# Four-layer sequence block: residual sums on TensorE and ScalarE and a new order in the routing stage

## The reference

```python
x = L0_attn_x                                                # (16, 256, 128)
x = x + attention(layernorm(x), Wqkv, bqkv, Wout, bout)      # softmax, 16 heads of 8
x = x + recurrent(layernorm(x), wf, uf, bf, wi, ui, bi, wc, uc, bc, wo, uo, bo, in_c)
x = x + linear_attention(layernorm(x), w_qkv, w_out)         # rope, elu + 1 features, 16 heads
x = x + experts(layernorm(x), Wr, br, W1, b1, W2, b2)        # the best two of 16 experts
```

```python
def step(c, xt):
    ft = sigmoid(xt @ wf.T + c @ uf.T + bf)
    it = sigmoid(xt @ wi.T + c @ ui.T + bi)
    gt = tanh(xt @ wc.T + c @ uc.T + bc)
    return ft * c + it * gt, None
h = tanh(x @ wo.T + c_final @ uo.T + bo)
```

```python
logits = x @ Wr + br
w, idx = top_k(softmax(logits), 2); w = w / sum(w)
y = sum over the two of w * (gelu(x @ W1[e] + b1[e]) @ W2[e] + b2[e])
```

## Time and profile before

| | |
|---|---|
| median of 3 runs | 697.38 us (693.48 to 697.74) |
| profiled execution | 696.24 us, its span 694.4 us |
| TensorE busy | 505.3 us, 73% of the span |
| VectorE busy | 432.5 us, 62% |
| GpSimd busy | 392.0 us, 56% |
| ScalarE busy | 348.8 us, 50% |

### The profile page before, as it was taken

The page is one execution under the profiler, slowest core; times in us unless marked ns, Lnnn a source line. Parts: engine busy times, 40 slices in busy tenths (PEclk is TensorE's granted clock), DMA queues, the critical chain, the costliest instruction groups (busy, mean ns, idle before and its releaser), DMA issues.

```text
span 694.4 us, 15346 instructions
## 1 busy us (share of the span) xinstructions
PE 505.3 (73%) x4146; PEld 345.2 (50%) x4146; DVE 432.5 (62%) x1259; ACT 348.8 (50%) x765; POOL 392.0 (56%) x692
## 2 busy tenths in 40 slices
PE   1468899999999999876777776766514776977730
PEld 0224555555555555444455555544414776877620
DVE  5467888888788888422478888887543344443306
ACT  1027777777777777752256545553322443444310
POOL 4555777776777753433215676677760665556550
PEclk9999999999999999997599999998555998989875
DMA  2864444343343331000700000000022222222119
GB/s 73 229 151 107 110 118 103 96 100 98 105 105 92 100 97 48 5 1 1 248 0 24 26 27 27 23 31 29 31 74 67 79 79 69 72 79 67 56 30 342
DMA packets 64092, 55.91 MB, mean 81 GB/s; under 512 B 8462, under 2 KB 56739, under 8 KB 64035
## 3 DMA queue, kind: packets, MB, share of 16 engines
q1 hardware_dynamic: 57986, 46.03, 25.0%
q0 software_dynamic: 4608, 8.47, 3.7%
q10 hardware_dynamic: 1440, 0.73, 0.4%
HBM read 30.53 MB, written 25.71 MB: 81 GB/s over the span
## 4 chain that ended last, share of the span: by engine, by line
PE 17%; issue 10%; POOL 7%; DVE 6%; another core or an unknown queue 3%; ACT 3%; DMA 3%; SPq 2%; POOLq 1%; DVEq 0%; ACTq 0%
PE p_qkv L1680 5%; POOL disp L1027 3%; POOL root L1045 2%; PE p_u L1693 1%; DMA own<-back 1%; PE p_kvo L1693 1%; PE p_qkv L1439 1%; ACT hid L1653 1%; PE p_r L1693 1%; PE p_qkv L1440 1%; PE p_h L1693 1%; POOL gap L1072 1%; DVE t L1133 1%; PE p_u L1447 1%
## 5 line engine op out<-in xcount | busy, mean ns | idle before, releaser
L422 DVE TENSOR_REDUCE negmax<-p_dve 128x4 f32<-128x1024 f32 x128 | 155.9, 1221 | 42.9 <-PE p_dve L612 41.5
L515 ACT ACTIVATE probs<-p_exp 128x1024 f32<-128x1024 f32 x128 | 130.7, 1021 | 28.4 <-PE p_exp L589 27.9
L1567 POOL DMA_INDIRECT back<-XN2T,rows x80 | 80.9, 1012 | 73.1 <-DVE XN2T L1627 49.0
L1027 POOL DMA_INDIRECT disp<-pay,pos x64 | 67.2, 1051 | 36.5 <-issue 18.4
L603 PE MATMUL p_out<-probs,V 128*32 128x256 f32 x1024 | 68.5, 385 | 0.0
L1653 ACT ACTIVATE hid<-p_qkv,own 128x128 f32<-128x128 f32 x160 | 45.6, 372 | 36.6 <-PE p_qkv L1680 16.6
L612 PE MATMUL p_dve<-KS,QS 61*128 61x256 bf16 x512 | 52.6, 287 | 13.1 <-DVE negmax L422 8.1
L1680 PE MATMUL p_qkv<-XN2T,own 128*128 128x128 f32 x320 | 48.4, 300 | 13.0 <-ACT XN2T L1645 10.1
L589 PE MATMUL p_exp<-QS,KS 64*128 64x256 bf16 x512 | 50.8, 277 | 8.5 <-ACT probs L515 4.4
L1680 PEld LDWEIGHTS p_qkv<-XN2T,own 128*128 128x128 f32 x320 | 44.3, 214 | 15.1 <-issue 13.5
L1619 DVE COPY own<-expert 128x514 f32 x80 | 35.7, 447 | 12.0 <-issue 11.9
(11 more groups left out here) (246 smaller groups left out, 1281.1 us busy)
## 6 DMA issues: line engine op xcount, KB each, us to landing
scratch<-part SPq DMA_DIRECT2D x32, 192.0 KB, 2.1
KS<-scratch SPq DMA_DIRECT2D x32, 192.0 KB, 3.3
QS<-scratch SPq DMA_DIRECT2D x32, 192.0 KB, 4.3
rows<-disp SPq DMA_DIRECT2D x80, 65.0 KB
scratch<-part SPq DMA_DIRECT2D x32, 128.0 KB, 2.0
own<-back SPq DMA_DIRECT2D x8, 512.0 KB, 6.6
expert<-in_W_dram SPq DMA_DIRECT2D x1, 2064.0 KB, 8.9
scratch<-part SPq DMA_DIRECT2D x32, 64.0 KB, 1.9
```

Of the source, the lines that this page charges most:

```text
L422: dve.tensor_reduce(negmax[q][:, i, :, 2 * hp:2 * hp + 2], p_dve[buf][:, :].rearrange("p (v w k) -> p v w k", v=HALF, k=S), AX.X, ALU.max, ...
L515: act.activation(probs[s % 4][:, :, :, :].rearrange("p v w q -> p (v w q)"), p_exp[:, :], ACT.Exp)\
L1027: pool.indirect_dma_start(out=disp, out_offset=bass.IndirectOffsetOnAxis(ap=pos[q][:, i, k:k + 1], axis=0), in_=pay[q][:, k, i, :], in_off ...
L1567: pool.indirect_dma_start(out=back, out_offset=bass.IndirectOffsetOnAxis(ap=rows[r][:, h, D + 1:ROW].bitcast(U32), axis=0), in_=y[r][:, h, :],
```

## The change

Eight edits, six of them in the routing stage:
1. The seven later loads of stage 1 are issued by ScalarE behind its first copies of q and k, no longer by SyncE.
2. In slot 2 of stage 1, where no attention weights are left to apply, TensorE does the blocks for VectorE before those for ScalarE.
3. `pipeline()` of the routing stage writes all turns out; there is no hardware loop.
4. `gap` is gone: ScalarE makes the exponential from `best` itself, one instruction for each of the two token tiles, with the second value as bias and the first scaled by -1.
5. `sent` becomes two semaphores, one for each set of buffers, and GpSimd no longer waits for the scatters of the turn before.
6. `uoh` is made by VectorE, no longer by GpSimd.
7. Both residual sums are made in the bank: TensorE multiplies with the identity instead of transposing, and adds X as a second product with the identity. ScalarE copies the sum from the bank to X. VectorE's two adds are gone.
8. Every engine has a new order in a turn.

```diff
+            def later_loads():
+                act.dma_start(X[:, 8:2 * B, :], t["x_dram"].rearrange("(n p) d -> p n d", p=P)[:, 8:2 * B, :]).then_inc(x_in[3].sem, 16)
+                act.dma_start(bo[:, :], t["bout"].partition_broadcast(P)).then_inc(w_in.sem, 16)
+                act.dma_start(Wout[:, :], t["Wout"]).then_inc(w_in.sem, 16)
...
+                        if at(n, 0):
+                            later_loads()
...
-                    for_act(n, r, s)
-                    for_dve(n, r, s)
+                    if s == 2 and not active(n, 2):
+                        for_dve(n, r, s)
+                        for_act(n, r, s)
+                    else:
+                        for_act(n, r, s)
+                        for_dve(n, r, s)
...
-        x4T_p, x4T_s, lg_p, lg_s, gap_s, odds_s = sig("x4T_p"), sig("x4T_s"), sig("lg_p"), sig("lg_s"), sig("gap_s"), sig("odds_s")
+        x4T_p, x4T_s, lg_p, lg_s, odds_s = sig("x4T_p"), sig("x4T_s"), sig("lg_p"), sig("lg_s"), sig("odds_s", TT)
         top_s, hot_s, pay_s = sig("top_s", 4), sig("hot_s"), sig("pay_s", 2)
-        rank_p, pos_s, sent = sig("rank_p"), sig("pos_s", 4), sig("sent", 16 * TT * TOP)
+        rank_p, pos_s = sig("rank_p"), sig("pos_s", 4)
+        sent = [sig(f"sent{q}", 16 * TT * TOP) for q in range(PAIR)]
...
-            peel = deepest + PAIR
-            rounds = (B - peel) // PAIR
-            for n in range(peel):
-                iteration(n, n % PAIR)
-            with eng.Fori(0, rounds, 1) as k:
-                for c in range(PAIR):
-                    iteration(k * PAIR + (peel + c), (peel + c) % PAIR)
-            for n in range(peel + rounds * PAIR, B + deepest):
+            for n in range(B + deepest):
...
-            pool.tensor_scalar(uoh[:, :], w["uo"][:, :], 0.5, None, ALU.mult).then_inc(s2.sem, 1)
...
-                                        in_=pay[q][:, k, i, :], in_offset=None).then_inc(sent.sem, 16)
+                                        in_=pay[q][:, k, i, :], in_offset=None).then_inc(sent[q].sem, 16)
...
-                    if sent.due(b - 1):
-                        pool.wait_ge(sent.sem, sent.at(b - 1))
                     steady(pool, t)
                     scatter(o, 0, 0)
+                root_power(n, r)
                 if active(n, 5):
                     scatter(o, 0, 1)
-                root_power(n, r)
                 if active(n, 5):
                     scatter(o, 1, 0)
                 if active(n, 5):
                     scatter(o, 1, 1)
                 if active(n, 4):
                     b = n - 4
-                    pool.wait_ge(top_s.sem, top_s.at(b, TT))
-                    if odds_s.due(b - 1):
-                        pool.wait_ge(odds_s.sem, odds_s.at(b - 1))
-                    pool.tensor_tensor(gap[:, :], best[:, :, 1], best[:, :, 0], ALU.subtract).then_inc(gap_s.sem, 1)
+                    pool.wait_ge(nm4.sem, nm4.at(b))
+                    steady(pool, t)
+                    pool.tensor_tensor(X[:, bass.ds(2 * b, 2), :], X[:, bass.ds(2 * b, 2), :], pay[r][:, 0, :, 0:D], ALU.add)\
+                        .then_inc(res.sem, 1)
                 if active(n, 4) and not (isinstance(n, int) and n - 4 < PAIR):
                     b = n - 4
-                    pool.wait_ge(sent.sem, sent.at(b - PAIR))
+                    pool.wait_ge(sent[b % PAIR].sem, sent[b % PAIR].at(b // PAIR - 1))
                     steady(pool, t)
                     pool.tensor_scalar(pay[r][:, :, :, D + 1].bitcast(I32), pay[r][:, :, :, D + 1].bitcast(I32), float(PAIR * TOP * TT), None, ALU.add)\
                         .then_inc(ids_up.sem, 1)
-                if active(n, 5):
-                    b = n - 5
-                    pool.wait_ge(nm4.sem, nm4.at(b))
-                    steady(pool, t)
-                    pool.tensor_tensor(X[:, bass.ds(2 * b, 2), :], X[:, bass.ds(2 * b, 2), :], pay[o][:, 0, :, 0:D], ALU.add)\
-                        .then_inc(res.sem, 1)
 
             pipeline(pool, iteration, 5)
             then["pool"](pool)
...
+                    dve.wait_ge(w["loaded"].sem, w["loaded"].at(0))
+                    dve.tensor_scalar(uoh[:, :], w["uo"][:, :], 0.5, None, ALU.mult).then_inc(mv_set.sem, 1)
...
-                    dve.tensor_tensor(X[:, bass.ds(2 * b, 2), :], p_u[:, 0:S].rearrange("p (i d) -> p i d", i=TT), X[:, bass.ds(2 * b, 2), :], ALU.add)\
-                        .then_inc(x3_s.sem, 1)
...
-                    dve.tensor_tensor(X[:, bass.ds(2 * b, 2), :], p_h[:, 0:S].rearrange("p (i d) -> p i d", i=TT), X[:, bass.ds(2 * b, 2), :], ALU.add)\
-                        .then_inc(x2_s.sem, 1)
...
-                    act.wait_ge(gap_s.sem, gap_s.at(b))
...
+                if active(n, 1):
+                    b = n - 1
+                    act.wait_ge(hT_p.sem, hT_p.at(b))
+                    if at(b, 0):
+                        act.wait_ge(s2.sem, 4)
+                        act.wait_ge(fill_set.sem, fill_set.at(0))
+                    act.activation(X[:, bass.ds(2 * b, 2), :], p_h[:, 0:S].rearrange("p (i d) -> p i d", i=TT), ACT.Identity,
+                                   bias=w["fill"][:, 0:1], scale=KVones[0][:, 0, D:D + 1]).then_inc(x2_s.sem, 1)
...
+                    act.wait_ge(top_s.sem, top_s.at(b, TT))
                     if gate_in.due(b - 1):
                         act.wait_ge(gate_in.sem, gate_in.at(b - 1))
-                    act.activation(odds[:, 1, :], gap[:, :], ACT.Exp).then_inc(odds_s.sem, 1)
+                    for i in range(TT):
+                        act.activation(odds[:, 1, i:i + 1], best[:, i, 0:1], ACT.Exp, bias=best[:, i, 1:2], scale=-1.0).then_inc(odds_s.sem, 1)
...
+                    act.wait_ge(u_p.sem, u_p.at(b))
+                    act.wait_ge(nm3.sem, nm3.at(b))
+                    act.activation(X[:, bass.ds(2 * b, 2), :], p_u[:, 0:S].rearrange("p (i d) -> p i d", i=TT), ACT.Identity,
+                                   bias=w["fill"][:, 0:1], scale=KVones[0][:, 0, D:D + 1]).then_inc(x3_s.sem, 1)
...
+                    pe.wait_ge(onT3_s.sem, onT3_s.at(b))
+                    pe.wait_ge(x2_s.sem, x2_s.at(b))
+                    if x3_s.due(b - 1):
+                        pe.wait_ge(x3_s.sem, x3_s.at(b - 1))
+                    for i in range(TT):
+                        pe.matmul(p_u[:, i * P:(i + 1) * P], on3T[:, i * P:(i + 1) * P], w["Wout2"][:, :], start=True, stop=False)
+                        mm = pe.matmul(p_u[:, i * P:(i + 1) * P], ident[:, :], X[:, 2 * b + i, :], start=False, stop=True)
+                    mm.then_inc(u_p.sem, 1)
...
+                    pe.wait_ge(h_s.sem, h_s.at(b))
+                    for i in range(TT):
+                        pe.matmul(p_h[:, i * P:(i + 1) * P], hT[o][:, i * P:(i + 1) * P], ident[:, :], start=True, stop=False)
+                        mm = pe.matmul(p_h[:, i * P:(i + 1) * P], ident[:, :], X[:, 2 * b + i, :], start=False, stop=True)
...
-                    for i in range(TT):
-                        mm = pe.matmul(p_u[:, i * P:(i + 1) * P], on3T[:, i * P:(i + 1) * P], w["Wout2"][:, :], start=True, stop=True)
...
-                    turn(p_h, hT[r][:, :].rearrange("p (i d) -> p i d", i=TT)).then_inc(hT_p.sem, 1)
...
-        if t["sent"].due(B - 1):
-            sp.wait_ge(t["sent"].sem, t["sent"].at(B - 1))
+        for q in range(PAIR):
+            sp.wait_ge(t["sent"][q].sem, t["sent"][q].at(B // PAIR - 1))
```

434 lines of the change are left out of this document (212 added, 222 removed).

## The result

The changed kernel takes 687.44 us (median of four runs, 685.41 to 687.78) against 696.75 us (693.48 to 697.74): a ratio of 0.9859 with a 95% interval of 0.9831 to 0.9888. In a later session the two stood at 687.73 and 698.30, 0.9823 (0.9767 to 0.9878). The forecast was 678.6, with a range from 671 to 689. A difference of 1.4% is small, but the interval leaves no room for none.

What follows compares the result with a forecast made beforehand. VectorE and GpSimd waiting for each other once per routing turn was taken as the bound. Gains of 13.0 (turns), 3.3 (drain), 0 (ramp), 1.5 (loads), 1.0 (stage 1's end) made 18.8: 697.4 to 678.6 us, range 671 to 689.

Steps and rivals of the forecast that it cites:

- rival 1: Routing stage: the chain through TensorE and ScalarE takes over, turns of 9.1 to 9.8 us, 690 us in all; chance 0.12.
- A turn of 8.6 us: Routing stage: a full turn from one `pos` to the next takes 8.6 us, bounds 8.1 to 9.1, instead of 9.96.
- this adds up to 0.5: Routing stage: GpSimd's add of X and `pay` holds up some VectorE instruction, adding up to 0.5 us to a turn.
- GpSimd idle 1 us before the first scatter: Routing stage: a sign of being right, GpSimd idle about 1 us before the first scatter of a turn.
- 2 us for the clock: Eleven full routing turns: 2 us added for stretches in which TensorE's clock falls to 1.2 GHz.
- rival 3: Routing stage: slower because TensorE stays at 1.2 GHz, about half the turns or more, 704 us or more; chance 0.05.
- Drain, 3.3 us: Last four turns of the routing stage: 31.5 us instead of 34.8, a gain of 3.3, bounds 1 and 5.
- The loads, 1.5 us with 0 as the lower bound: Head of stage 1: later loads issued by ScalarE instead of SyncE gain 1.5 us, bounds 0 and 2.5.
- The end of stage 1, 1.0 us: End of stage 1: TensorE turns the second half of `OT` before `xn`, gaining 1.0 us, bounds 0.5 and 1.2.
- The loop, 2.6 us: Routing stage: the hardware loop costs some 0.65 us a pair, 2.6 in four pairs, contained in the turn length.
- rival 2: Routing stage: `z` still waits for a late exponential, only the loop and first-stage gains are won, 692 us; chance 0.06.
- All alike: Routing stage: a sign of being right, marks of `pos` 8.3 to 8.9 us apart in the middle and all alike.

## Why the prediction came out as it did

The direction and the range held; the gain was 9.3 us where 18.8 stood. The time lies near the upper end of the range, outside the 671 to 686 that the forecast gave to its own mechanism and inside the 686 to 693 of rival 1. The mechanism is the forecast's all the same. What failed are sizes: the add that fell on `z` (0.85 us a turn where 0.25 was taken), the landings that `pay` waits for (put at nothing), and the loads (a loss where a gain stood). The total agrees better than its parts, which miss in both directions.

- **A turn of 8.6 us.** Measured 8.9 (8.7 to 8.94). The chain was the right one: the way to the root took 3.66 us (3.5 to 4.0 forecast), VectorE's wait for it 0.34 us. VectorE's own part took 5.24 instead of 4.6 us. The step of it that was mis-sized is the GpSimd add, "this adds up to 0.5", of which half was taken: it cost 0.85. Without it the part would be 4.39 us, as short as forecast, and with the add elsewhere there are turns of 8.07 to 8.24 us (two buffers) and 8.12 to 8.17 (fourteen). Over eleven turns 3.3 us. "Up to 0.5" was the delay that one instruction had met; what a delay costs depends on where the add starts.
- **GpSimd idle 1 us before the first scatter.** Measured 1.46 us. This was named as a sign of being right, and is where the picture was incomplete: some of it is no slack. With four buffers GpSimd's queue alone filled 8.88 us, with 0.77 us ahead of the first scatter. The changed kernel has 1.46 us there, 0.7 more, so the queue did not set its ordinary turns, but it stands close behind and caps a better order. The working had counted GpSimd's instructions and not the gaps between them.
- **2 us for the clock.** In this trace the turn with a mean of 0.70 is 2.3 us longer than an ordinary one and that with 0.75 0.3 us. But the first began with a wait of 1.75 us for a landing, before the clock fell, so that the clock's share is smaller and not known. That the sum comes near 2 is no confirmation. What was held against rival 3, that TensorE would be busier, goes with what the traces show.
- **A wait that the sum did not have.** `pay` waited for scatters to land, 1.75 us in the turn of 11.2 and some 1 us in that of 10.4, which are 2.3 and 1.5 us longer than an ordinary one. The prediction said that no row shows GpSimd waiting for a store, which is so; but ScalarE's `pay` waits for one too, and in the new order it stands closer behind the scatters. It could have been read before, in the last turns of the old kernel (0.48 and 0.96 us; this is the second):

```profile
505.37 1.09 ACT L1324 ACTIVATE pay<-X,root 128x256 f32<-128x256 f32 x2 [0.96 <-DMA disp<-pay,pos]
```

Four and fourteen buffers show what it cost: no such turn is left.

- **Drain, 3.3 us.** Measured 0.8. The last turn, forecast at 6.6 us because `gap` is gone, took 8.95: the last `pay` waited 3.30 us, for the same landing. With fourteen buffers that turn takes 4.52 us.
- **The loads, 1.5 us with 0 as the lower bound.** Measured -1.9 us at the maxima in this pair, and -0.6 to -2.5 between all traces of either kind. The working named the shared DMA engines and then set the bound at zero; the writes that left 3.8 us earlier landed later than before. The kernels with the loads elsewhere confirm the place of it. This is the one step with the wrong sign.
- **The end of stage 1, 1.0 us.** Measured 1.4 to 1.7 in this trace. At the last add the gain is there in all traces (1.0 to 2.0); to the end of the recurrence this trace is the shortest of twelve and seven of the others show no gain, so the good agreement here is luck.
- **The loop, 2.6 us.** Measured alone as 3.3 (1.5 to 5.7): more per pair than forecast, with a part lost again to the clock.
- **The rivals.** TensorE's chain (rival 1) does not set the turn: four more passes, of 0.44 us, leave turns of 8.0 us possible. Its time, 690 us, came near the measured one by other causes. `z` did not wait for the exponential in any turn (rival 2), and the clock fell in two of eleven turns, where rival 3 needed half of the time.
- **The signs named.** The root directly behind the first scatter and VectorE's wait of 0.34 us for it came true in the ordinary turns. "All alike" did not: in the two long turns VectorE waited 1.1 to 1.9 us at a time for TensorE's `p_kvo`. The maxima from 38.5 us and the last add of X 3.5 us earlier did not come either; the add came 0.6 us later, at 315.12.

Sum of the differences in this trace: 3.3 us by the turn, 2.3 by the two long turns beyond the 2 us allowed, 2.5 by the drain, 3.4 by the loads, 0.6 by the ramp, less 0.7 from the end of stage 1 and 1.4 behind the last `pos`: 10.0, of the 18.8 - 8.7 = 10.1 us that the spans lack. Two of these, 0.7 and 1.4, are smaller than what the two traces of the changed kernel differ by in the same stretches (1.7 and 2.9 us); they balance the sum and explain nothing.

## What to carry to other kernels

When an engine's queue is counted, the short gaps between its instructions belong to it: a GpSimd turn of 7.1 us of work was a full 8.9 us. A small GpSimd instruction that is left in a turn must be followed to where it will fall; moved from one place to another it cost 0.39, 0.45, 0.49 or 0.85 us on one VectorE instruction. And for every buffer ask who waits for its readers, on all engines: the double buffer was free for GpSimd and was waited for by ScalarE, and to give it more room brought 6 to 8.5 us, where the whole change brought 9 to 11. And a long turn with a lower clock in it need not be the clock's: look at what the engines waited for before the clock fell.

## What the runs showed of the hardware beyond that

- Beside GpSimd's add of 128x256 (0.70 us alone), VectorE's sum of two numbers per partition took 1.00 us instead of 0.15, its add of 128x512 1.18 instead of 0.67, and the GpSimd add itself 1.13.
- A bias spread over partitions took 4.93 us to issue on SyncE; on ScalarE its issue took 3.70 us.
- In the chain of waits of the changed kernel the landing of a turn's last scatter, counted from its start, stands five times: 2.40, 2.43, 2.50, 3.00 and 3.91 us.
- The kernel before took 669.59 us on one chip and 698.30 and 701.12 on two others. In the traces of kernels like the changed one 27 to 35 us of such a difference lie in the stage of the experts. TensorE was busy 89 to 90 us there on the faster chip and 98 to 102 on the others, and the DMA engines moved 119 to 120 GB/s instead of 95 to 98. TensorE's clock alone thus does not account for it; the cause is open.
